# Second attention: its first tiles normalised inside the gated FFN, gate rows of half two built a pair sooner, and the last FFN's weight maxima taken during the gated FFN

## What is computed

```
x = x + tanh(g_xattn[0]) * differential_attention(layernorm(x), ctx)      # stage 1: 16 heads
x = x + tanh(g_ffn[0]) * gated_ffn(layernorm(x))                          # stage 2: ternary weights, 8-bit activations
# stage 3, 4 heads of 64:
q, k, v = layernorm(x), ctx, ctx;  cat = concatenate([q, k, v])
ig = cat @ igate_kernel + igate_bias;  fg = cat @ fgate_kernel + fgate_bias
cs = cumsum(log_sigmoid(fg))                                              # over the tokens
log_D = where(causal, cs - cs.T, -inf) + ig.T;  m = max(log_D, -1)
C = (q @ k.T / 8) * exp(log_D - m)
h = C / (maximum(abs(sum(C, -1)), exp(-m)) + 1e-6) @ v
x = x + tanh(g_xattn[1]) * headwise_norm(h) * outnorm_scale
# stage 4, per-tensor scales: the largest |w1|, |w2|, |x| and |h| set them
x = x + tanh(g_ffn[1]) * qlinear(gelu(qlinear(layernorm(x), w1, b1)), w2, b2)
```

## Time and profile before

| | us |
|---|---|
| median of three runs | 1303.05 |
| lowest, highest | 1301.57, 1304.61 |
| the profiled execution | 1300.35 |
| its span | 1298.5 |
| busy in it: TensorE | 1187.1 (91%) |
| VectorE | 1107.8 (85%) |
| ScalarE | 999.8 (77%) |
| POOL | 837.0 (64%) |

### The profile page before, as it was taken

The page is one execution under the profiler, slowest core; times in us unless marked ns, Lnnn a source line. Parts: engine busy times, 40 slices in busy tenths (PEclk is TensorE's granted clock), DMA queues, the critical chain, the costliest instruction groups (busy, mean ns, idle before and its releaser), DMA issues.

```text
span 1298.5 us, 30931 instructions
## 1 busy us (share of the span) xinstructions
PE 1187.1 (91%) x11672; PEld 851.3 (66%) x11672; DVE 1107.8 (85%) x1812; ACT 999.8 (77%) x1725; POOL 837.0 (64%) x1316
## 2 busy tenths in 40 slices
PE   4699999999999999999998999998799888389898
PEld 3367777777777777777764666666678676244387
DVE  3488989899999998888879899987649899979977
ACT  2388888888887887878876999997455665699895
POOL 3158687777868778686776888776117786877100
PEclk9999999999999999999999999999999889699999
DMA  9677788778778787676420000001545364055089
GB/s 154 118 154 144 168 172 150 149 145 171 155 163 151 147 182 128 131 131 118 91 61 1 1 2 1 1 2 46 189 133 134 84 182 112 1 230 224 1 351 362
DMA packets 126659, 163.61 MB, mean 126 GB/s; under 512 B 47522, under 2 KB 79394, under 8 KB 123042
## 3 DMA queue, kind: packets, MB, share of 16 engines
q1 hardware_dynamic: 125744, 160.85, 52.8%
q10 hardware_dynamic: 768, 0.79, 0.5%
HBM read 76.59 MB, written 33.03 MB: 84 GB/s over the span
## 4 chain that ended last, share of the span: by engine, by line
PE 50%; POOL 15%; DVE 14%; ACT 9%; issue 6%; DMA 3%; SPq 2%; ACTq 0%; DVEq 0%; POOLq 0%
PE psum L615 7%; PE psum L630 6%; PE psum L2208 4%; PE psum L597 4%; PE psum L1084 4%; PE psum L585 3%; POOL rs L935 3%; PE psum L642 3%; ACT f_gelu L2264 3%; PE psum L660 3%; PE psum L1125 3%; POOL a_fac L1929 2%; PE psum L560 2%; PE psum L1619 2%; SPq L431 2%
## 5 line engine op out<-in xcount | busy, mean ns | idle before, releaser
L743 ACT ACTIVATE exp_t<-psum 128x512 f32<-128x512 f32 x512 | 278.6, 599 | 98.4 <-PE psum L615 98.4
L815 DVE TENSOR_REDUCE neg_max<-psum 128x8 f32<-128x1024 f32 x256 | 312.7, 1221 | 31.2 <-PE psum L597 24.5
L935 POOL TENSOR_TENSOR rs<-rs,minus_half 128x16 f32<-128x16 f32 x64 | 187.2, 2925 | 5.0
L615 PEld LDWEIGHTS psum<-q_stack,k_stack 50*128 50x128 f32 x2048 | 133.4, 186 | 74.6 <-ACT exp_t L743 39.5
L615 PE MATMUL psum<-q_stack,k_stack 50*128 50x128 f32 x2048 | 169.7, 285 | 0.5 <-ACT exp_t L743 0.5
L630 PE MATMUL psum<-exp_t,v_pad 128*32 128x256 f32 x2048 | 137.0, 385 | 0.4 <-DVE x_state L846 0.4
L597 PE MATMUL psum<-k_stack,q_stack 48*128 48x256 f32 x1024 | 119.1, 310 | 19.2 <-DVE neg_max L815 16.5
L1084 PE MATMUL psum<-f_w,f_xqt 128*128 128x512 bf16 x512 | 121.4, 379 | 1.9 <-DVE f_hid L1245 1.4
L927 POOL TENSOR_TENSOR sq<-u 128x256 f32<-128x256 f32 x64 | 39.2, 613 | 116.8 <-DVE u L836 116.8
L106 DVE BATCH_NORM_STATS2 norm_stats<-x_state 128x6 f32<-128x256 f32 x256 | 101.8, 411 | 11.5 <-DMA x_state<-in_x 11.5
L1929 POOL TENSOR_TENSOR a_fac<-a_fac,a_expo 128x16 f32<-128x16 f32 x16 | 52.3, 3270 | 74.3 <-DVE a_fac L1835 73.9
(11 more groups left out here) (257 smaller groups left out, 3002.9 us busy)
## 6 DMA issues: line engine op xcount, KB each, us to landing
k_stack<-k_hi SPq DMA_DIRECT2D x252, 128.0 KB, 4.4
k_stack<-k_lo SPq DMA_DIRECT2D x126, 128.0 KB, 4.5
g_scratch<-f_gelu SPq DMA_DIRECT2D x14, 1024.0 KB, 4.5
f_gelu<-g_scratch SPq DMA_DIRECT2D x9, 1024.0 KB, 13.1
ctx_t<-in_ctx_t SPq DMA_DIRECT2D x32, 256.0 KB, 5.2
x_state<-in_x SPq DMA_DIRECT2D x16, 512.0 KB, 6.7
v_in<-in_ctx SPq DMA_DIRECT2D x32, 256.0 KB, 4.5
v_scratch<-v_in SPq DMA_DIRECT2D x32, 256.0 KB, 4.7
```

The source lines that it names most:

```text
L615: r = e.matmul(psum[:, bank + j, o:o + P], self.k_st[rows, b // 2 % self.NK, pair // 2 % 2, pair % 2, i, pair // 4, b % 2, :], self.q_st[r ...
L743: e.activation(self.prob[:, n % 3, j].rearrange("p n w t -> p (n w t)"), psum[:, self.score_bank(n) + j, :], ACT.Exp).then_inc(s["exp"], 1)
L815: e.tensor_reduce(self.negm[:, b % 2, :, :, 2 * u:2 * u + 2].rearrange("p j w n -> p j n w"), psum[:, 0:2, :].rearrange("p j (n w k) -> p ...
L935: e.tensor_tensor(self.rs[:, i], self.rs[:, i], self.expo[:, :], ALU.pow).then_inc(s["pool"], 1)
```

## The change

It does the following.
- VectorE adds the gate weights (`dve_gate_weights`) and normalises tiles 0 to 7 of stage 3 (`dve_normalise`) inside stage 2's last steps, 64 to 71. `begin` is cut in two: TensorE, ScalarE and SP start after `open` (the last hidden tile made) and come to `begin` later: TensorE ahead of the gates, ScalarE behind its warming activation, SP behind the first two context groups and the placing table.
- POOL no longer clears a_m_row, nor a_v as a whole (it sets one column per head and the rest behind them); the three m rows lie at 24 to 26 directly behind the 24 a rows, so nothing between needs zeros, and a_a_row is set to ones in rows 0 to 31. The matmul L1596 reads 27 rows, not 35.
- Half one: tiles 42 and 43 come ahead of the first split; the second split is POOL's. Half two: copy at pair 10, scan at pair 11, both splits by POOL at pair 12. The filler matmuls of pairs 13 and 14 go.
- `add(i-5)` moves behind `next_max(i-12)` in VectorE's pair.
- The weight maxima are taken during stage 2, from a load of both weights into the unused region (2 x 1 MB, issued at the end of stage 1), in four pieces of 1024 columns behind steps 18, 26, 34 and 42; in pair 22 one small reduce joins them. The later load stays. The two roundings go to ScalarE, at the ends of pairs 29 and 30.

```diff
--- stage 2, SP and VectorE
+            if tick == self.a0.END - 1:
+                self.fw.load_first(w)
...
+            if b in self.NEXT_MAX_AT:
+                self.fw.dve_piece_max(w, self.NEXT_MAX_AT.index(b))
...
+    NEXT_NORMED = {NSEQ + 1: (0,), NSEQ + 2: (1,), NSEQ + 3: (2,), NSEQ + 4: (3,), NSEQ + 6: (4, 5), NSEQ + 7: (6, 7)}
+    NEXT_MAX_AT = [18, 26, 34, 42]
...
                 step(b)
+                if b == NSEQ:
+                    self.a1.dve_gate_weights(w)
+                for n in self.NEXT_NORMED.get(b, ()):
+                    self.a1.dve_normalise(w, n)
--- Attention1
+    def open(self, w):
+        w.wait_ge(self.f0.s["hid"], NSEQ)
+    def dve_normalise(self, w, b):
+        self.f0.wait_rounded(w, NSEQ - 8)
+        self.sh.wait_rstd(w, 2, b)
+        w.wait_ge(self.s["qt_pe"], b // 2 - 1)
+        self.sh.normed(w.e, self.xn[:, b % 4], b).then_inc(self.s["xn"], 1)
+    def parts_made(self, w, hf):
+        w.wait_ge(self.s["parts"], 5)
+        w.wait_ge(self.s["init"], self.INIT + (15 if hf else 5))
--- its sp
         w.wait_ge(s["load"], self.WEIGHTS)
-        self.begin(w)
+        self.open(w)
...
         load_group(0)
+        w.wait_ge(self.f0.a0.s["v_out"], 16 * self.NP)
         e.dma_start(self.place, t["gate_rows"][:, :, :]).then_inc(s["load"], 16)
         load_group(1)
+        self.begin(w)
...
-            w.wait_ge(s["parts"], 10 * hf + 10)
+            self.parts_made(w, hf)
--- its pe
-        self.begin(w)
+        self.open(w)
...
         def gates(g):
+            self.begin(w)
...
-                r = e.matmul(psum[:, 2 + b, :], self.a_row[0:35, p % 2, :], ...
+                r = e.matmul(psum[:, 2 + b, :], self.a_row[0:27, p % 2, :], ...
...
-            if i in (13, 14):
-                w.wait_ge(s["scan"], 9)
-                keep_busy(6, 6)
--- its act
-        self.begin(w)
+        self.open(w)
         e.activation(self.warm[:, :], sh.ones[:, 0:1], ACT.Exp).then_inc(s["log_f"], 1)
+        self.begin(w)
...
-            if i == 11:
+            if i in (29, 30):
+                self.fw.act_round(w, i - 29)
+            if i == 10:
                 log_forget(1)
--- its dve
-        for b in range(4 * self.EARLY):
+        for b in range(8, 4 * self.EARLY):
             normalise(b)
...
             if b == 41:
                 scan(0)
+            if b == 43:
                 self.three_parts(w, 0, 0)
-                self.three_parts(w, 0, 1)
                 maximum(0)
...
-            if 0 <= i - 5 < self.NP:
-                add(i - 5)
             if 0 <= i - 4 < self.NP:
                 scale(i - 4)
...
                 next_max(i - 12)
+            if 0 <= i - 5 < self.NP:
+                add(i - 5)
...
+            if i == 10:
+                log_forget(1)
             if i == 11:
-                log_forget(1)
-            if i == 12:
                 scan(1)
                 maximum(1)
-            if i in (22, 23):
-                self.fw.dve_max(w, i - 22)
+            if i == 22:
+                self.fw.dve_max(w)
...
-            if i in (28, 29):
-                self.fw.dve_round(w, i - 28)
--- its pool
-        e.memset(self.v_aug[:, :, :], 1.0).then_inc(s["init"], 1)
-        e.memset(self.a_row[:, :, :], 0.0).then_inc(s["init"], 1)
-        e.memset(self.m_row[:, :, :, :, :], 0.0).then_inc(s["init"], 1)
-        w.wait_ge(s["init"], 4)
-        e.memset(self.a_row[32:35], 1.0).then_inc(s["init"], 1)
+        e.memset(<the column behind each head's values in v_aug>, 1.0).then_inc(s["init"], 1)
+        e.memset(self.v_aug[:, :, 2 * NH * (self.HD + 1):], 1.0).then_inc(s["init"], 1)
+        e.memset(self.a_row[0:32], 1.0).then_inc(s["init"], 1)
...
+        self.three_parts(w, 0, 1)
         for i in range(self.NP + 6):
...
-            if i in (12, 13):
-                self.three_parts(w, 1, i - 12)
+            if i == 12:
+                self.three_parts(w, 1, 0)
+                self.three_parts(w, 1, 1)
--- Ffn1Weights
+    def load_first(self, w):
+        t, into = self.sh.t, self.a0.tw.next_w
+        w.wait_ge(self.a0.s["st_pe"], 4 * NSEQ)
+        w.wait_ge(self.a0.s["s_pe"], 4 * NSEQ)
+        for i, name in enumerate(("w1_t", "w2_t")):
+            w.e.dma_start(into[:, i] ..., t[name] ...).then_inc(self.s["load"], 16)
+    def dve_piece_max(self, w, k):
+        i, h = divmod(k, 2)
+        w.wait_ge(self.s["load"], self.FIRST)
+        w.e.tensor_reduce(self.sh.next_wmax[:, k:k + 1], self.a0.tw.next_w[:, i, 1024 * h:1024 * h + 1024], AX.X, ALU.max, ...)
+    def dve_max(self, w):
+        w.wait_ge(self.s["dve"], 4)
+        w.e.tensor_reduce(self.wmax[:, :], <the four pieces' maxima>, AX.X, ALU.max).then_inc(self.s["dve"], 1)
-    def dve_round(self, w, i):
+    def act_round(self, w, i):
+        w.wait_ge(self.s["load"], self.LOADED)
         w.wait_ge(self.s["dve"], self.INV)
-        w.e.tensor_scalar(self.w32[i][:, :], self.w32[i][:, :], self.swi[:, i:i + 1], ROUND, ALU.mult, ALU.add)
+        w.e.activation(self.w32[i][:, :], self.w32[i][:, :], ACT.Copy, scale=self.swi[:, i:i + 1], bias=ROUND)
```

More of the change, by code:

```diff
@@ L1451, in three_parts @@
         s, e, rest = self.s, w.e, self.gates[:, hf, 0] if kind else self.t1[:, hf]
-        n = 10 * hf + 5 * kind
-        w.wait_ge(s["scan"], 8 * hf + 7)
+        made = s["init" if hf or kind else "parts"]
+        n = self.INIT + (5 * (kind + 1) if hf else 0) if hf or kind else 0
+        w.wait_ge(s["scan"], 8 * hf + 6 + (not kind))
         for i in range(3):
-            w.wait_ge(s["parts"], n + 2 * i)
-            e.tensor_copy(self.parts[:, hf, kind, i, :], rest).then_inc(s["parts"], 1)
+            w.wait_ge(made, n + 2 * i)
+            e.tensor_copy(self.parts[:, hf, kind, i, :], rest).then_inc(made, 1)
             if i < 2:
-                w.wait_ge(s["parts"], n + 2 * i + 1)
-                e.tensor_tensor(rest, rest, self.parts[:, hf, kind, i, :], ALU.subtract).then_inc(s["parts"], 1)
+                w.wait_ge(made, n + 2 * i + 1)
+                e.tensor_tensor(rest, rest, self.parts[:, hf, kind, i, :], ALU.subtract).then_inc(made, 1)
+    def parts_made(self, w, hf):
+        w.wait_ge(self.s["parts"], 5)
+        w.wait_ge(self.s["init"], self.INIT + (15 if hf else 5))
     def kt_landed(self, w, p):
```

49 lines of the change are left out of this document (27 added, 22 removed).

## The result

The changed kernel took 1292.19 us in the median of 4 runs (1289.66 to 1293.46), the kernel before 1302.36 on the same chip (1301.57 to 1304.61): ratio 0.9919, 95% interval 0.9902 to 0.9935. It is faster, as forecast, but by 10 us where 20 were promised, and it lies 0.2 us above the upper end of the range. On another occasion the same changed kernel took 1289.65, ratio 0.9903 (0.9884 to 0.9922), inside the range.

What follows compares the result with a forecast made beforehand. TensorE bounds the FFN and first pairs, VectorE the pairs from 16 on. 5.3 + 4.1 + 3.2 + 7.3 + 0.6 − 0.4 = 20.1 us off the median 1303.05 gives 1283.0, range 1278 to 1292.

Steps and rivals of the forecast that it cites:

- Parts 1 and 2: Second attention's opening, fourth gate group sooner, gain 5.3 us; half one's gates, tiles 42 and 43 first, gain 4.1.
- The two terms that the text shows for tile 42: Half one: next gates move from 941.6 to 938.8; the group after takes 2.84 us or less instead of 3.7.
- Part 6: FFN: four weight maxima added to VectorE, mostly hidden in its waits; cost 0.4 us, bounds 0 and 4.8.
- Rival (a): The FFN pays the weight maxima in full, 4.8 us; total 1287.4; chance 0.10.
- Part 3: Half two's gates, pairs 11 to 16: earlier scan and POOL sets end the row wait; gain 3.2 us, between 1 and 5.5.
- rival (e): A step does nothing: pair 16's rows stay late, the gain of Part 3 is lost; total 1286.2; chance 0.06.
- 25.3 are left, I allow 1.5 of waits: 26.8: Combine 11 to 16: VectorE's 25.95 us of work less the 0.65 copy, plus waits, instead of 29.97.
- Rival (b): POOL becomes the brake: 2.0 us lost in the opening, Part 3 gives nothing; total 1288.2; chance 0.08.
- Part 4: VectorE-bound late pairs: maxima and roundings removed 6.6 us, add moved 1.0, ScalarE cost 0.3; gain 7.3, bounds 5 and 8.8.
- rival (c): Late pairs hardly speed up, TensorE slips to the low clock and takes VectorE's place; total 1289.9; chance 0.10.
- Rival (d): Without fillers TensorE stays at 1.2 GHz from pair 12 on, kernel slower, up to 1355; chance 0.04.
- Part 5: Tail, pair 32: VectorE's wait of 1.55 us for POOL ahead of add shrinks; gain 0.6, 0 to 1.55.

Runs made afterwards that it cites:

- no_early: Changed kernel with tiles 0 to 7 normalised again at the start of the second attention; 1295.09 us, ratio 0.9939 to the kernel before.
- after: Profiled execution of the changed kernel itself, no further edit; 1293.46 us, against a median of 1292.19.
- again: The changed kernel run and profiled a second time, no edit; 1289.65 us, ratio 0.9903 to the kernel before.
- k35: Changed kernel with the three m rows back at rows 32 to 34, so the exponent matmul reads 35 rows; 1288.29 us, ratio 0.9893.
- fill2: Changed kernel with two filler matmuls on TensorE at the end of each of pairs 12 to 30; 1288.80 us, ratio 0.9895.
- add_back: Changed kernel with add(i-5) again ahead of scale(i-4) on VectorE; 1289.59 us, ratio 0.9916.
- fill2_add: Changed kernel with two filler matmuls in each of pairs 12 to 30 and add(i-5) again ahead of scale(i-4); 1288.40 us, ratio 0.9897.
- round_back: Changed kernel with the two roundings again on VectorE, in pairs 28 and 29; 1289.47 us, ratio 0.9906.
- fill2_round: Changed kernel with two filler matmuls in each of pairs 12 to 30 and the roundings again on VectorE; 1290.80 us, ratio 0.9914.
- scan_back: Changed kernel with half two's copy at pair 11, scan at 12, POOL's sets at 12 and 13, no fillers; 1289.53 us, ratio 0.9909.
- best: Changed kernel with 35 rows in the exponent matmul, two fillers a pair and add ahead of scale; 1289.94 us, ratio 0.9914.

## Why the prediction was half right

**Parts 1 and 2, the opening and the gates of half one: right.** 9.4 forecast, 9.3 measured (61.03 to 51.72), and event by event: fourth group 5.35 sooner (5.3), tile 42 3.95 (4.1). The two terms that the text shows for tile 42, 2.8 and 0.9, come to 3.7 and not to 4.1; they measured 3.20 and 0.75. no_early agrees with the share given to the early tiles and, as far as it goes, with that of POOL's clearing. The rule quoted against part 2 (SBUF — State Buffer, Who interferes with whom, in the Trainium skill), by which 2.0 would be lost, did not bite at that place: POOL's operations end at 934.8, before the next normalisations (935.31, 1.37 for four). It holds where it was not applied, see below.

**Part 6, the FFN: right, and even cheaper.** −0.1 measured for a cost of 0.4. Rival (a) falls: the maxima came out of the 11.0 us of waits.

**Left out: the smaller exponent matmul.** The diff's change of 35 to 27 rows was in no term of the sum. "The first pairs of the attention proper are again TensorE's" is the sentence where it belonged: in a stretch whose bound is TensorE every edit of a matmul has to be priced. Measured: 1.6 to 2.1 of the 1.8 to 2.3 that were lost there.

**Part 3: mechanism right, size wrong.** The row wait of 4.21 is gone (rival (e) falls), but the step "25.3 are left, I allow 1.5 of waits: 26.8" failed. VectorE was busy 27.39, not 25.3, since a scale (1.75), an a_fac (1.30), an a_scan (1.34) and an a_den (0.67, its like take 0.16 and 0.25) were held up beside POOL's scaled, and it waited 1.7, of which 1.32 for POOL's factor. The gain was 0.9, within the bounds given (1 to 5.5) but for a tenth; the lower bound, that POOL's one piece costs what the late rows did, is nearly what happened. Rival (b) had this half right: no gain from part 3, but nothing lost in the opening.

**Part 4: two of three terms right, one off, one missing.** Roundings 2.04 (2.1), reorder 1.1 (1.0), both with the clock held. The reorder's figure is in part luck: the forecast took 1.0 of 1.2 us of waits, and the runs show 2.4 of waits gone against 1.3 of busy time that came in. Maxima 2.7 instead of 4.2, as 1.7 of held-up instructions came in with them out. By the busy time: 4.5 of maxima and 2.6 of roundings left VectorE, its busy time fell only from 76.19 to 72.80, 3.4. The rest is the growth of a_hn and a_fac, 3.0 (10.4 + 3.3 to 12.2 + 4.5), and of the one a_exp_m, 0.95; as durations, which overlap a little, they come to slightly more than the 3.7 that are missing. The waits of 2.49 fell to 0.52. Together 5.4 with the clock held, for 7.3; undone one at a time the three come to 5.8, so they do not simply add. Then the clock: rival (c), with a probability of 0.10, happened in part and in some executions.

| kernel (same late pairs but for the edit named) | granted clock, combine 16 to 31 | us |
|---|---|---|
| after | 0.83 | 77.00 |
| again | 0.93 | 74.18 |
| k35 | 0.88 | 73.45 |
| no_early | 0.93 | 73.33 |
| fill2 | 1.00 | 73.32 |
| add_back / fill2_add | 0.83 / 0.98 | 77.34 / 74.42 |
| round_back / fill2_round | 0.84 / 1.00 | 78.19 / 75.36 |

At 0.88 and more the low clock costs 0 to 0.9, as TensorE has slack (in k35 0.2 a pair more than in the others); at 0.83 and 0.84 it costs 2.8 to 3.7. In after's profile the low level covers 1047.0 to 1064.0 without a break, three and a half pairs, and in those of add_back and round_back as long a piece; the other profiles have within the late pairs single drops of 3.4 to 6.8, or none. The text had named a mean clock under 0.85 in the pairs as a sign that it was wrong, and that sign came. The forecast's "TensorE's 69.80 busy is 4.65 a pair, it stays just under" took the mean; it is the long drop that crosses VectorE's pace: in after VectorE waits 4.7 for TensorE's scores in four places, up to 3.1 at once, in again 0.4. Rival (d) falls: the clock always came back.

**Part 5: wrong sign.** 0.6 forecast, 0.6 to 1.0 lost. The wait of 1.55 is gone indeed. Changed kernel, VectorE at pair 32:
```profile
1107.54 1.74 DVE L1872 TENSOR_TENSOR a_hn<-a_num,a_fac 128x512 f32<-128x512 f32 x1 [0.35 <-POOL a_fac L1955]
```
Scale, which now comes first, is released by the end of POOL's factor at the moment at which POOL's own scaled starts: it waits 0.35 and then loses 1.06. With `add` first again and the fillers the tail takes 38.10 instead of 38.62, and with the roundings on VectorE 38.25: each accounts for 0.4 to 0.5 of the loss. The same kernel alone gave 38.78 and 38.37, so these are small figures; but 38.10 came three times with `add` first and fillers, and 38.61 or 38.62 in k35, fill2 and scan_back.
The Trainium skill (SBUF — State Buffer, Who interferes with whom) has this as a lock held for a whole instruction, which a VectorE operation with two SBUF inputs also meets. The runs agree: 0.68 becomes 1.74 beside a POOL instruction of 1.26, and what grows is a scale, an a_fac or an a_den, all with two inputs. Besides them a_scan and a_exp_m grow, which have one; the moments, the maxima, the sums a_ssq and combine ran beside the same scaled and did not (0.40 to 0.42, 0.66, 0.67 and 1.20 to 1.23). In the forecast I tried the rule only where the diff moved POOL's work (part 2), not where it moved VectorE's work onto POOL's.

**The sum.** Forecast 20.1; measured in after's profile against before's: 9.3 − 1.8 + 0.9 + 1.7 − 1.0 + 0.1 = 9.2 in the forecast's stretches, less 2.1 lost before the FFN (3.0 and −0.9), 7.1 of span. The second profile gives 11.8 there, and 6.4 lost before the FFN. That loss at the start I can't explain: the code there is the same in all kernels, yet the first stretch took 58.3 to 58.7 in four profiles (before, k35, fill2, fill2_add) and 59.9 to 62.9 in ten, with the low clock in five of them and at 1.00 throughout in the other five (best, 62.26). Nor is it settled what lets the clock fall for 17 us in one execution of a program and not in the next.
